# The end of the attention in another order, in a gated cross-attention and mixture-of-experts kernel

## The reference

```
h   = layernorm(x)
x   = x + tanh(g0) * attention(h, ctx, ctx, mask)       # 16 heads of width 64
z   = layernorm(x)
p   = sigmoid(z @ router.T + bias); the two best of 8 experts, their p scaled to sum 1
x   = x + tanh(g1) * (shared_ffn(z) + sum over the two experts of p_e * ffn_e(z))
ffn = (silu(z @ gate) * (z @ up)) @ down                 # inner width 256
```

## Time and profile before

| | |
|---|---|
| median of three runs | 176.14 us |
| the profiled execution, its own time | 176.26 us |
| its span, first to last instruction | 174.4 us |
| time outside the span | 1.86 us |
| mean granted clock of TensorE, share of full | 0.995 |
| PE busy, share of the span | 92% |
| DVE, ACT, POOL busy | 73%, 64%, 63% |

### The profile page before, as it was taken

One profiled execution on the slowest core, in us unless ns is written; L12 is line 12 of the kernel. 1 busy time (PEld: TensorE's weight loads), 2 busy tenths in 40 slices (PEclk: granted clock), 3 DMA queues, 4 the chain that ended last, 5 costly groups with the idle time before them and its releaser, 6 DMA issues.

```text
span 174.4 us, 4611 instructions
## 1 busy us (share of the span) xinstructions
PE 159.9 (92%) x1412; PEld 139.5 (80%) x1412; DVE 127.6 (73%) x612; ACT 111.3 (64%) x427; POOL 110.0 (63%) x139
## 2 busy tenths in 40 slices
PE   7799889999999999999999996997899999999970
PEld 7687669998898998898998875895677788887860
DVE  2689988665989597878597978478784777776283
ACT  3666997774868774868774968651665566665300
POOL 3675799854869744768724768567644566666621
PEclk9999999999999999999999999999999999999997
DMA  5899996730000000000000000001414223211172
GB/s 164 267 368 379 414 401 241 284 136 4 15 2 0 19 2 4 31 17 19 31 4 0 16 21 16 17 26 40 109 40 118 64 78 83 67 52 41 53 244 91
DMA packets 11096, 17.35 MB, mean 99 GB/s; under 512 B 2075, under 2 KB 6945, under 8 KB 10944
## 3 DMA queue, kind: packets, MB, share of 16 engines
q1 hardware_dynamic: 9504, 14.59, 24.3%
q0 software_dynamic: 1280, 2.20, 3.9%
q10 hardware_dynamic: 288, 0.26, 0.4%
HBM read 9.99 MB, written 7.51 MB: 100 GB/s over the span
## 4 chain that ended last, share of the span: by engine, by line
PE 47%; POOL 14%; ACT 14%; issue 12%; DMA 6%; DVE 4%; SPq 1%; DVEq 0%; POOLq 0%
ACT probs L727 8%; PE misc L411 8%; POOL ys L1449 7%; PE pt L385 5%; PE o_bank L400 5%; PE s_even L374 5%; PE proj_q L331 3%; DMA wq_raw<-wqT 3%; PE proj_k L331 3%; PE proj_k L333 3%; PE proj_k L332 3%; PE proj_q L333 2%; PE proj_q L332 2%; DMA probs<-ys 2%; POOL xs L1369 2%
## 5 line engine op out<-in xcount | busy, mean ns | idle before, releaser
L727 ACT ACTIVATE probs<-probs,negmax 128x128 f32<-128x128 f32 x128 | 49.9, 393 | 18.8 <-DVE negmax L937 18.7
L1339 POOL TENSOR_TENSOR probs<-probs,rinv 128x512 f32<-128x512 f32 x32 | 33.0, 1047 | 19.6 <-DVE rinv L951 19.5
L1449 POOL DMA_INDIRECT ys<-probsT,places x23 | 22.5, 979 | 15.0 <-ACT places L852 12.9
L727 ACT ACTIVATION_READ_ACCUMULATOR probs<-probs,negmax 128x1 f32 x128 | 24.2, 189 | 0.0
L937 DVE CUSTOM_DVE_ANT_0 probs<-s_even,mask 128x128 f32<-128x128 f32 x64 | 18.1, 283 | 5.2 <-issue 5.2
L1369 POOL DMA_INDIRECT xs<-xrow,slot x16 | 16.3, 1021 | 6.8 <-issue 3.9
L385 PE MATMUL pt<-ident_sb,probs 128*128 128x128 f32 x128 | 17.6, 277 | 1.7 <-POOL probs L1339 1.1
L374 PE MATMUL s_even<-kT,qT 64*128 64x128 f32 x128 | 18.5, 284 | 0.4 <-DVE negmax L937 0.4
L374 PE MATMUL s_odd<-kT,qT 64*128 64x128 f32 x128 | 18.5, 285 | 0.0
L374 PEld LDWEIGHTS s_even<-kT,qT 64*128 64x128 f32 x128 | 15.4, 187 | 3.5 <-issue 1.2
L937 DVE CUSTOM_DVE_ANT_0 probs<-s_odd,mask 128x128 f32<-128x128 f32 x64 | 18.1, 283 | 0.0
(11 more groups left out here) (282 smaller groups left out, 454.8 us busy)
## 6 DMA issues: line engine op xcount, KB each, us to landing
xs<-pad SPq DMA_DIRECT2D x5, 858.0 KB, 6.6
xg<-xs SPq DMA_DIRECT2D x23, 66.0 KB, 1.9
down_sb<-down SPq DMA_DIRECT2D x1, 1152.0 KB, 9.7
probs<-ys SPq DMA_DIRECT2D x4, 256.0 KB, 3.9
gu_raw<-gu SPq DMA_DIRECT2D x3, 256.0 KB, 5.8
wk_raw<-wkT SPq DMA_DIRECT2D x2, 256.0 KB, 4.0
wq_raw<-wqT SPq DMA_DIRECT2D x2, 256.0 KB, 5.0
mask<-mask SPq DMA_DIRECT2D x8, 64.0 KB, 1.9
```

What stands on the lines that cost most here:

```text
L727: e = act.activation(probs[:, r, l, :], probs[:, r, l, :], ACT.Exp, bias=negmax[:, r, l:l + 1], scale=-1.0, accum_out=rowsum[:, r, l:l + 1])
L1339: pool.tensor_tensor(quad, quad, rinv[:, r, 4 * u:4 * u + 4].unsqueeze(2).to_broadcast([P, 4, P]), ALU.mult).then_inc(norm_done, 1)
L1449: pool.indirect_dma_start(out=ys, out_offset=bass.IndirectOffsetOnAxis(ap=places[:, n:n + 1].bitcast(U32), axis=0), in_=y_sb[n % IN_FLIGHT ...
```

## The change

The change reorders the hand-written end of the attention, and the loop's second half, on all engines:

- `x2_raw` becomes two buffers. ACT copies the transposed rows once, to `x2_raw` (`x2_copy`); the high part (`x2_hi`) and DVE's low part (`x2_lo`) are made from that copy. `logits` waits no longer for the low part. The logits of batches 6 and 7 go to the banks of their transposes, not to a score bank.
- The norm of the odd batch has its statistics ahead of the mask of group g+6 in the loop, its rows amid that mask; POOL's root comes ahead of the scatters. After the loop, the second quad of group 14 (`exps`, `recips`) comes behind the copy and the transposes of routing group 2.
- PE transposes and makes logits of group 2 ahead of `values(13)`, and ranks ahead of both quads of group 15. Batch 7's rows come behind the choice and the weights of batch 6 on DVE.
- At the first blocks `ranks(LAST)` stands behind the first block's gate and up, and the choice of batch 7 ends behind the first `block_lo`.

Line numbers of the changed kernel are one lower on PE, 5 or 6 lower in parts of PE and ACT, and 9 to 12 higher on DVE and POOL.

The diff, without the renaming of `lg_bank` in `route_exp` and without what the order rows above show of the loop's last lines:

```diff
-        x2_raw = sb("x2_raw", [P, 2, P])
+        x2_raw = [sb(f"x2_raw{i}", [P, 2, P]) for i in range(2)]
...
-        lg_bank = route_bank[:3] + [s_bank[1], s_bank[1]]
...
             def logits(r):
                 pe.wait_ge(x2raw_ready, r + 1)
-                if r < 3:
-                    pe.wait_ge(x2lo_ready, r + 1)
-                if r == 3:
-                    pe.wait_ge(ttr_done, 8 * GROUPS)
...
             transposes(13, 1)
+            x2_transposes(2)
             scores(15, last, 3)
+            logits(2)
             values(13, last, 1)
-            x2_transposes(2)
             transposes(14, 2)
-            logits(2)
             out_project(B - 2, use)
-            transposes(15, 3, (0,))
             pe.wait_ge(ez_ready, 3)
             ranks(2)
-            transposes(15, 3, (1,))
+            transposes(15, 3)
             values(14, last, 2)
             values(15, last, 3)
+            x2_transposes(3)
             out_project_half(B - 1, use + 1, 0)
-            x2_transposes(3)
+            logits(3)
             out_project_half(B - 1, use + 1, 1)
-            logits(3)
             pe.wait_ge(gulo_ready, EXPERTS)
-            pe.wait_ge(table_ready, 1)
-            experts = {n: block_expert(n) for n in range(2)}
             pe.wait_ge(counts_read, 1)
             shared_pass(0, 0)
             shared_pass(0, 1)
-            x2_transposes(LAST)
             pe.wait_ge(ez_ready, 4)
             ranks(3)
+            pe.wait_ge(table_ready, 1)
+            experts = {n: block_expert(n) for n in range(2)}
+            x2_transposes(LAST)
             stay_warm(1)
             logits(LAST)
...
+            def x2_copy(r):
+                act.wait_ge(x2t_done, r + 1)
+                if r >= 2:
+                    act.wait_ge(lg_done, r - 1)
+                    act.wait_ge(x2lo_ready, r - 1)
+                tiles = len(ROUTED[r])
+                act.copy(x2_raw[r % 2][:, 0:tiles, :].rearrange("p t d -> p (t d)"),
+                         route_bank[r][:, P:(1 + tiles) * P]).then_inc(x2raw_ready, 1)
+
+            def x2_hi(r):
+                act.wait_ge(x2raw_ready, r + 1)
+                tiles, first = len(ROUTED[r]), ROUTED[r][0]
+                act.copy(xn2T_hi[:, first * P:(first + tiles) * P],
+                         x2_raw[r % 2][:, 0:tiles, :].rearrange("p t d -> p (t d)")).then_inc(x2hi_ready, 1)
...
-                dve.tensor_tensor(xn2T_lo[:, cols], route_bank[r][:, P:(1 + tiles) * P], xn2T_hi[:, cols].bitcast(F32),
-                                  ALU.subtract).then_inc(x2lo_ready, 1)
+                dve.tensor_tensor(xn2T_lo[:, cols], x2_raw[r % 2][:, 0:tiles, :].rearrange("p t d -> p (t d)"),
+                                  xn2T_hi[:, cols].bitcast(F32), ALU.subtract).then_inc(x2lo_ready, 1)
...
                 add_attention(2 * p + 1, use + 1)
                 steps = norm2_steps(2 * p + 1, use + 1)
-                mask_max(g + 6, p + 1, 2, islice(steps, 2))
+                run(steps, 2)
+                mask_max(g + 6, p + 1, 2, after(4, run, steps, 1))
+                recips(g + 6, 2, (0,))
                 copy_o(g + 4, 0)
-                recips(g + 6, 2, (0,))
-                run(steps, 1)
-                recips(g + 6, 2, (1,))
+                if p < PAIRS - 2:
+                    recips(g + 6, 2, (1,))
...
             copy_pt(13, 1)
-            mask_max(15, PAIRS - 1, 3)
+            mask_max(15, PAIRS - 1, 3, after(6, recips, 14, 2, (1,)))
             copy_o(13, 1)
-            x2_lo(2)
-            recips(15, 3, (0,))
             choice = choose_steps(2)
             run(choice, 2)
+            recips(15, 3, (0,))
+            finish(choice)
             recips(15, 3, (1,))
-            finish(choice)
...
+            x2_lo(2)
             x2_lo(3)
...
             choice = choose_steps(3)
-            run(choice, 4)
+            run(choice, 3)
+            finish(choice)
+            finish(weight_steps(3))
             run(norm, 1)
-            finish(choice)
+            place(3)
             finish(norm)
-            finish(weight_steps(3))
             x2_lo(LAST)
-            place(3)
...
-            finish(choose_steps(LAST))
+            choice = choose_steps(LAST)
+            run(choice, 3)
             block_lo(0)
+            finish(choice)
             finish(weight_steps(LAST))
+            block_lo(1)
             place(LAST)
-            block_lo(1)
...
                 normalise(4 * p + 5, 1)
+                rstd_second(2 * p + 1)
                 if p:
-                    scatter(p - 1, 1, 2)
-                rstd_second(2 * p + 1)
-                if not p:
+                    scatter(p - 1, 1, 3)
+                else:
                     split_expert(5)
                 normalise(4 * p + 6, 2)
                 if p:
-                    scatter(p - 1, 2, 4)
+                    scatter(p - 1, 3, 4)
...
             scatter(2, 1, 4)
+            count_chosen(2)
             rstd_second(B - 1)
-            count_chosen(2)
             count_chosen(3)
```

More of the change, by code:

```diff
@@ L450, in logits @@
                 for i in range(len(ROUTED[r])):
-                    at_col = lg_bank[r][:, 384 + E_ROUTED * i:384 + E_ROUTED * (i + 1)]
+                    at_col = route_bank[r][:, 384 + E_ROUTED * i:384 + E_ROUTED * (i + 1)]
                     pe.matmul(at_col, ident_sb[:], bias_sb, start=True, stop=False)
-                    mm = pe.matmul(at_col, x2_raw[:, i, :], router_sb[:], start=False, stop=True)
+                    mm = pe.matmul(at_col, x2_raw[r % 2][:, i, :], router_sb[:], start=False, stop=True)
                 mm.then_inc(lg_done, 1)
@@ L668, in _ @@
             pe.wait_ge(in_down, 16)
+            block_transpose(1)
+            block_gate_up(0, experts[0])
             pe.wait_ge(ez_ready, LAST + 1)
             ranks(LAST)
-            block_transpose(1)
-            block_gate_up(0, experts[0])
             for n in range(BLOCKS):
@@ L741, in copy_o @@
                 act.copy(oT[:, r % 2, :, :].rearrange("p c q -> p (c q)"), o_of.get(g, o_bank)[:]).then_inc(ot_ready, 1)
-            def x2_split(r):
[L745 to L751, removed]
+            def x2_copy(r):
[11 more added lines that the diff above has]
+                         x2_raw[r % 2][:, 0:tiles, :].rearrange("p t d -> p (t d)")).then_inc(x2hi_ready, 1)
+            def x2_split(r):
+                x2_copy(r)
+                x2_hi(r)
             def route_exp(r):
@@ L757, in route_exp @@
                 tiles = len(ROUTED[r])
-                act.activation(ez[:, 0:tiles, :].rearrange("p t e -> p (t e)"), lg_bank[r][:, 384:384 + E_ROUTED * tiles], ACT.Exp,
+                act.activation(ez[:, 0:tiles, :].rearrange("p t e -> p (t e)"), route_bank[r][:, 384:384 + E_ROUTED * tiles], ACT.Exp,
                                scale=-1.0).then_inc(ez_ready, 1)
@@ L824, in _ @@
                 exps(g + 6, 2, 0)
-                exps(g + 6, 2, 1)
+                if p < PAIRS - 2:
+                    exps(g + 6, 2, 1)
             def silu(unit):
@@ L833, in _ @@
             copy_pt(13, 1)
+            x2_copy(2)
+            exps(14, 2, 1)
+            route_exp(2)
             exps(15, 3, 0)
-            x2_split(2)
-            exps(15, 3, 1, lambda: route_exp(2))
+            exps(15, 3, 1)
             copy_pt(14, 2)
@@ L840, in _ @@
             copy_pt_late(15, 3)
+            x2_hi(2)
             copy_o(14, 2)
```

## The result

The changed kernel takes 178.2 us in the median of four runs (177.81 to 179.49); the kernel before took 176.06 beside it. The ratio is 1.0136, with a 95% interval of 1.0081 to 1.019: slower, where faster was forecast, and outside the predicted range of 174.4 to 176.7 us.

The account below looks back on a forecast made before the run. PE's unchanged blocks bound the kernel, with block 5 set by the later of PE's stream and the last scatter's gather. Block 5 0.4 to 0.9 us earlier, middle 0.65, loop at 0: 175.5 us median, 175.2 to 175.75; whole range 174.4 to 176.7.

Parts of the forecast that it names:

- X: Start of the first `xg_lo`, ahead of the first block's gate and up: 124.00 before, forecast 1.4 to 1.9 us earlier.
- the clock: Rival: PE idles more between 117 and 122.5 us, its clock may fall to 1.2 GHz: 177 to 178 us, chance 0.04.
- Edits without a sum: Loop: statistics ahead of the mask, rows amid it, copies; put at 0, with 0.2 us gained to 0.4 lost.
- What comes back: First blocks: late `ranks(LAST)` loses one us of lead on the scatter's route, 0.2 on PE's; block 5 0.4 to 0.9 earlier.
- What bounds the kernel: PE's unchanged blocks, full from 138 to 160 us; the change is worth what it moves them by, through block 5.
- Logits of group 2: Placed right behind group 15's scores; their exponential `ez` comes at 106.2, 3.9 us earlier.
- Exponentials of group 15: All eight run on ACT from 106.3 to 109.5, 1.9 us earlier; POOL's second quad starts at about 110.0.
- To batch 7's rows: On DVE, behind batch 6's choice and weights: 2.6 to 2.7 us behind the sum, 1.7 to 1.2 us earlier.
- The price of that neighbourhood: Group 2's weights on DVE beside POOL's normalise of group 15: nothing, or up to 0.45 us later.
- To batch 7's sum: From group 15's second quad through values and projection to DVE's add: at 116.0 instead of 117.95, 1.95 us earlier.
- The lead is eaten by POOL: Rival: POOL goes ahead of group 2's `hot`, steps behind come 0.4 to 0.9 later: 176.1 us, chance 0.20.
- To X: From batch 7's rows: 1.84 us to its `ez`, now about 0.2 less; the table load behind stays; X at 122.6 to 122.1.

Follow-up runs that it names:

- the fillers: Five warm-keeping matmuls in each of TensorE's two idle stretches, added to the changed kernel: 177.03 us, ratio 1.0031 to the kernel before; three per stretch in later versions.
- the first turn: Batch 1's rows written behind the mask in the loop's first turn; added to the changed kernel with five fillers: 176.72 us, 1.0012; taken back from all three: 176.09 us, 1.0015.
- all three: Changed kernel plus three fillers per idle stretch, batch 1's rows behind the first turn's mask, and batch 7's ranks ahead of the first gate and up: 175.32 us, ratio 0.9947.
- without ranks first: The version with all three, but with batch 7's ranks again behind the first gate and up, in the changed kernel's VectorE order: 175.99 us, ratio 0.9995.
- rows behind the mask: Changed kernel with batch 1's rows written behind the mask, in the loop's first turn only: 177.85 us, ratio 1.0032 to the kernel before.
- last run: All three, with batch 7's rows ahead of batch 6's choice and weights, its root ahead of the count, its logits ahead of batch 6's ranks, nine fillers: 174.65 us, 0.9927.
- ranks first: Changed kernel with `ranks(LAST)` ahead of the first gate and up again, and VectorE's order to match: 177.91 us, ratio 1.0067 to the kernel before.
- split moved: Changed kernel with POOL's split of the sixth expert moved from beside the first turn's mask to behind the next normalise: 177.39 us, ratio 1.0045.
- without fillers: The version with all three, less its warm-keeping matmuls in TensorE's idle stretches: 176.58 us, ratio 1.001 to the kernel before.

## Why the prediction was wrong, step by step

Against the version with all three, each edit taken back costs, by the ratios: the fillers 0.63%, the first turn 0.68%, the ranks 0.48%, about 1.1, 1.2 and 0.85 us. Together that is 1.79%; the changed kernel is 1.89% above that version (1.0136 against 0.9947, the first known to half a per cent). So the three cover the loss, within the intervals. How it is shared out is less sure. The fillers' share was taken where the clock fell in 7 of 12 runs, and in the changed kernel it fell in 4 of 4. Added one by one to the changed kernel, the fillers bring 1.05% and the first turn on top of them only 0.19% (1.0031 to 1.0012), in a set with much spread.

With all three the change is worth 0.93 us. That is not the forecast's 0.65 come true, for X is 0.94 us earlier (123.06 for 124.00) and not 1.4 to 1.9. Nearest to what was forecast is the run without ranks first, with the clock held and the loop mended: there block 5 comes 0.38 us earlier (131.28), close to the forecast's 0.4 to 0.9, but by luck. X's lead was 0.95, and 0.57 of it was lost on PE's stream, not one us on the scatter's route.

*Failed: the clock.* The rival named what came, with a chance of 0.04; that its 177 to 178 lies near the measured 178.2 is partly luck, for it has neither the loop's loss nor the queue's in it. The step that failed is its last sentence: no stretch of the old trace falls, so this one won't. The stretch it rested on had 1.50 us of work in 2.00, with fillers in it; the rival's own text put PE at about half the time now and went on. All four runs of the changed kernel had a mean clock of 0.967 to 0.980, and the old kernel's clock fell, too, in most runs, once its fillers were out.

*Failed: Edits without a sum.* The loop was put at 0, with 0.4 as its worst; it lost 0.8. The rows amid the mask were looked at beside a scatter of the last round, not beside the split of an expert that POOL runs in the first, and their wait was taken at 0.5, not at a whole POOL instruction. ACT did not hide it, either: it takes the heads as the mask gives them. The trace of before showed the same instruction for batch 0 at 0.92 us, beside a split that POOL had begun at 45.09, but behind a mask and not amid it:

```profile
45.60 0.92 DVE L983 TENSOR_SCALAR xrow<-x_sb,moments,rstd 128x256 f32<-128x256 f32 x1
```

*Failed: What comes back.* "PE's stream loses only some 0.2" was 0.6 in the traces and 0.85 by the ratio. The scatter's route, which the forecast took for the later one, is late nearly as foretold (X + 2.4 with the clock held, for 2.6 to 2.7) and decides nothing: with the clock held no block 5 behind late ranks waited for its gather, even at X + 2.96. There 5.5 us from the scatter's start to block 5's weight load were enough (126.16 to 131.66); in the old trace it was 6.0, with a wait. Of the versions with late ranks one had that load wait: rows behind the mask, under a fallen clock, for 0.18 us. What was missed is the queue on VectorE: behind `place(LAST)`, which now waits for the late ranks, stand three table steps and the first block's product, and PE needs that product.

*Held.* What bounds the kernel: block 5 moved by 3.2 us and the end by 3.3. *Logits of group 2*: with the loop's 0.8 added, 107.0 was due and 106.83 came. *Exponentials of group 15*: the last head ends at 110.0 for 110.3, the second quad starts at 110.88 for 110.8, both again with the 0.8. *To batch 7's rows*: 2.53 us from sum to rows for 2.6 to 2.7; the last run shows that this order, the count ahead of the root and TensorE's order there together held back 0.6 us of X. Of the four signs of being wrong three came: X at 125.07, a block 5 that didn't wait, a loop late by 0.8; the distance from block 5 to the end held.

*The price of that neighbourhood* came at its upper bound and twice: `hot` 1.07 us beside the quad of 109.60, the weights 0.86 beside that of 110.88, for 0.23 in the old trace, where nothing ran beside them. So the first scatter is at 112.72, 0.6 behind the 112.1 due with the loop's loss, and *To batch 7's sum* late by as much: 117.44 for 116.8. That is the rival *The lead is eaten by POOL*, with its 0.4 to 0.9: POOL began 0.04 us ahead of `hot`. The Trainium skill, "SBUF — State Buffer", "Who interferes with whom", says that an instruction of VectorE with two SBUF inputs and a GpSimd instruction that reads SBUF exclude each other for a whole instruction. The trace agrees for both. It also names tensor_scalar among the instructions that can use both ports; the rows at 1.50 and 0.41 us agree. `x2_lo`, which by the rule joined the list, took 0.28 to 0.43 us, as before: no POOL arithmetic stood beside it, only scatters at 115.98 and 120.88, which cost it nothing.

*To X* was not reached by its own terms: from the rows to X it took 5.1 us, with the clock falling on the way. With the clock held it is 4.0 (119.06 to 123.06), 0.5 more than the 3.5 worked out; in the changed kernel the transpose of these rows started 0.36 us behind their end, before 0.05. The register loads of two experts stand there now, and with them moved the transpose follows at 0.05 again (last run); they were not moved alone, so that part stays open.

## What to carry to other kernels

When an order is changed so that the matrix engine idles more, count its busy time over the stretch, and put the fillers into the new gaps in the same edit: a clock that falls costs more here (1.7 us between the runs of one kernel) than the whole lead (0.9). When a wait is added, read what stands behind it in that engine's queue and who waits for it, before following the data that waits. And when an instruction moves, look at what the neighbouring engine does at the new place in every turn of the loop, the first one too.

## What the runs showed of the hardware

In the changed kernel's profiled run the granted clock fell with no single idle stretch of PE above 0.84 us in the ten us ahead of it, and it stayed at 0.50 for some ten us, in which PE was busy 1.23 of 2.00 us from 124 to 126 and 2.00 of 2.00 us in the other four stretches. The same kernel keeps its clock in some executions and not in others: without the added fillers the mean was 0.981 or less in 4 of 4, 11 of 12, 8 of 9, 4 of 6 and 7 of 12 runs of five kernels (the changed one, rows behind the mask, ranks first, split moved, without fillers); with them in none of 74, where it was 0.991 or more.

A VectorE instruction can be held through a POOL instruction that by the trace began after it: the rows of batch 1 started at 50.31, POOL's subtraction at 50.38 (POOL's spans are rough), and the rows ended at 51.81, 0.15 us behind its end. They took 1.50 or 1.51 us in all four traced kernels with the two side by side, and 0.41 where the split was moved.
